# The opening of a fused attention and feed-forward kernel, reordered: a constant built on VectorE, a low part on GpSimd, one weight scaling ahead of a tile's statistics

## What is computed

```python
def reference(x, W_q, W_kv, W_o, gate_w, up_w, down_w, gate_scale, up_scale, down_scale):
    # layernorm: (x - mean) / sqrt(var + 1e-5)
    a = layernorm(x)
    q  = (a @ W_q.T).reshape(B, S, 16, 32)
    kv = (a @ W_kv.T).reshape(B, S, 16, 32)
    qf, kvf = l2_normalize_complex(fft(q)), l2_normalize_complex(fft(kv))
    kvf = cumsum(kvf, axis=1)
    v = ifft(qf * kvf).real.reshape(B, S, D)
    x = x + v @ W_o.T
    f = layernorm(x)
    g = silu((f @ fp8(gate_w)) * gate_scale) * ((f @ fp8(up_w)) * up_scale)
    return x + (g @ fp8(down_w)) * down_scale
```

## Time and profile before

| | |
|---|---|
| median of 3 runs | 422.57 us (422.27 to 423.33) |
| span of the profiled execution | 419.2 us |
| TensorE busy | 411.5 us (98%) |
| VectorE busy | 281.3 us (67%) |
| ScalarE busy | 193.4 us (46%) |
| GpSimd busy | 102.5 us (24%) |
| share of TensorE in the chain that ended last | 95% |

### The profile page before, as it was taken

The page is one execution under the profiler, slowest core; times in us unless marked ns, Lnnn a source line. Parts: engine busy times, 40 slices in busy tenths (PEclk is TensorE's granted clock), DMA queues, the critical chain, the costliest instruction groups (busy, mean ns, idle before and its releaser), DMA issues.

```text
span 419.2 us, 5474 instructions
## 1 busy us (share of the span) xinstructions
PE 411.5 (98%) x1895; PEld 218.8 (52%) x1895; DVE 281.3 (67%) x497; ACT 193.4 (46%) x322; POOL 102.5 (24%) x108
## 2 busy tenths in 40 slices
PE   8999999999999999999999999999999999999994
PEld 4744454455455554554554564454555555555553
DVE  5999998999999694287676952186784744332234
ACT  3787656676755245546222573255342522122220
POOL 0133641015334322045350031043541001300003
PEclk9999999999999999999999999999999999999999
DMA  8986548600381144140112025320112041200002
GB/s 249 289 240 238 177 101 187 141 2 0 94 209 26 38 64 88 39 167 34 27 33 44 2 50 89 62 95 7 25 27 52 0 90 37 75 2 0 2 0 100
DMA packets 57546, 33.54 MB, mean 80 GB/s; under 512 B 49456, under 2 KB 49840, under 8 KB 57392
## 3 DMA queue, kind: packets, MB, share of 16 engines
q1 hardware_dynamic: 57088, 32.93, 30.7%
q10 hardware_dynamic: 432, 0.28, 0.2%
HBM read 17.44 MB, written 4.19 MB: 52 GB/s over the span
## 4 chain that ended last, share of the span: by engine, by line
PE 95%; DMA 1%; DVE 1%; SPq 1%; POOL 0%; POOLq 0%; issue 0%
PE bd L461 21%; PE bu L445 20%; PE bg L445 20%; PE ba L350 15%; PE ba L390 8%; PE bd L350 4%; PE ba L363 1%; DMA h<-x_dram 1%; PE bd L390 1%; PE bd L363 1%; PE bg L350 1%; PE bu L350 1%; PE bu L390 1%; PE bd L407 1%; PE bd L336 0%; PE bg L422 0%
## 5 line engine op out<-in xcount | busy, mean ns | idle before, releaser
L461 PE MATMUL bd<-dw,fu 128*128 128x512 f32 x376 | 100.0, 411 | 0.0
L445 PE MATMUL bu<-hT,gu 128*128 128x512 f16 x384 | 90.7, 379 | 0.0
L445 PE MATMUL bg<-hT,gu 128*128 128x512 f16 x376 | 89.2, 380 | 0.0
L461 PEld LDWEIGHTS bd<-dw,fu 128*128 128x128 f32 x376 | 70.6, 188 | 18.6 <-DVE fu L1165 0.7
L1160 DVE SCALAR_TENSOR_TENSOR ff<-bu,us,sl 128x512 f32<-128x512 f32 x48 | 35.9, 747 | 65.0 <-PE bu L445 61.8
L708 ACT ACTIVATE sl<-bg,gs 128x512 f32<-128x512 f32 x48 | 32.9, 686 | 80.2 <-PE bg L445 79.3
L350 PE MATMUL ba<-wf,xT 128*128 128x512 f16 x288 | 63.2, 379 | 0.0
L445 PEld LDWEIGHTS bu<-hT,gu 128*128 128x128 f16 x384 | 37.4, 98 | 45.6 <-DVE ff L1160 0.6
L445 PEld LDWEIGHTS bg<-hT,gu 128*128 128x128 f16 x376 | 34.1, 98 | 45.8 <-issue 8.9
L1165 DVE TENSOR_TENSOR fu<-ff,fu 128x512 fp32r<-128x512 f32 x47 | 40.1, 856 | 15.7 <-ACT fu L714 15.3
L1534 POOL TENSOR_TENSOR h<-ff,h 128x512 f32<-128x512 f32 x14 | 17.6, 1277 | 129.8 <-DVE ff L1186 129.8
(11 more groups left out here) (180 smaller groups left out, 449.9 us busy)
## 6 DMA issues: line engine op xcount, KB each, us to landing
h<-x_dram SPq DMA_DIRECT2D x16, 256.0 KB, 4.2
out_dram<-h SPq DMA_DIRECT2D x15, 256.0 KB, 2.0
hT<-w_q_dram SPq DMA_DIRECT2D x4, 256.0 KB, 3.8
gu<-w_kv_dram SPq DMA_DIRECT2D x4, 256.0 KB, 4.7
hT<-gate_w_dram SPq DMA_DIRECT2D x2, 512.0 KB, 3.8
hT<-up_w_dram SPq DMA_DIRECT2D x2, 512.0 KB, 5.9
gu<-woT_dram SPq DMA_DIRECT2D x1, 1024.0 KB, 5.5
hT<-down_w_dram SPq DMA_DIRECT2D x2, 512.0 KB, 5.0
```

The lines of the kernel that those rows point to most:

```text
L445: m = e.matmul(bk[:, :], gu[:, c, 4 * w + k, col:col + P], hT[:, b % 2, part, k, :], start=k == 0 and part == 0, stop=k == KT - 1 and part ...
L461: m = e.matmul(bd[t][:, :], fu_at(n)[:, part, P * t:P * t + P], dw[:, i, :], start=i == 0 and part == 0, stop=i == NI - 1 and part == 1)
```

## The change

It does the following, and nothing else:

- `heads` is no longer sent from the host. VectorE builds it after `dve_zero`: one memset of the 128 x 128 square to 0 and four memsets of 32 x 32 squares. The `cst` transfer has 128 instead of 256 columns. The first `pe_heads` waits for these five memsets, the first `dve_head` for the transfer.
- The low part of x's first tile is made by GpSimd (`pool_xl(0, 0)`) instead of VectorE.
- The 4 warm-up matmuls behind the second `pe_heads` are gone.
- On VectorE `dve_head(0, 1)` stands ahead of the statistics of tile 1; those of tile 2 stand behind `dve_head(1, 0)`, those of tile 3 behind `dve_head(1, 1)`.
- On SyncE all four w_kv quarters stand ahead of the transposes of x's first tile, x tile 2 behind them.
- The last waits of SyncE are in another order: those for the outputs of the last batch (d_o[0]) come last, tile 2 at the very end.

The diff, cut to its core:

```diff
-            if j == 0:
-                e.wait_ge(d_cst, 16)
+            if j == 0:
+                e.wait_ge(v_heads, 5)
...
+            if j == 0:
+                e.wait_ge(d_cst, 16)
...
+        def dve_heads(e):
+            e.memset(heads, 0.0).then_inc(v_heads, 1)
+            e.wait_ge(v_heads, 1)
+            for q in range(4):
+                r = slice(HD * q, HD * q + HD)
+                e.memset(cst[r, 128 + HD * q:128 + HD * q + HD], 1.0 / UNIT).then_inc(v_heads, 1)
...
             pe_heads(e, 0, 1)
-            pe_warm(e, 4)
             pe_fold(e, 0, 1)
...
             dve_zero(e)
+            dve_heads(e)
             dve_stats1(e, 0, 0)
...
             dve_head(e, 0, 0)
-            dve_xl(e)
             dve_sum_w(e, 2)
+            dve_head(e, 0, 1)
             dve_stats1(e, 0, 1)
             dve_root0_head(e, 0, [1])
-            dve_head(e, 0, 1)
             dve_root0_tail(e, 0, [1])
             dve_xn(e, 0, 1)
-            dve_stats1(e, 0, 2)
             dve_sum_w(e, 4)
...
             dve_head(e, 1, 0)
-            dve_stats1(e, 0, 3)
+            dve_stats1(e, 0, 2)
             dve_root0_head(e, 0, [2])
             dve_head(e, 1, 1)
+            dve_stats1(e, 0, 3)
             dve_root0_tail(e, 0, [2])
...
         def gpsimd_program(e):
+            pool_xl(e, 0, 0)
             pool_xl(e, 0, 1)
...
             sp_raw(e, 1, 1)
-            sp_x(e, 0, 2)
             sp_raw(e, 1, 0)
-            sp_xT(e, 0, 0)
-            sp_raw(e, 1, 2)
             sp_raw(e, 1, 3)
+            sp_raw(e, 1, 2)
+            sp_xT(e, 0, 0)
+            sp_x(e, 0, 2)
             sp_ident(e)
...
             for t in range(NT):
-                e.wait_ge(d_o[0][t], 16 * 2)
                 e.wait_ge(d_o[1][t], 16)
                 e.wait_ge(d_o[2][t], 16)
+            for t in (0, 1, 3, 2):
+                e.wait_ge(d_o[0][t], 16 * 2)
```

More of the change, by code:

```diff
@@ L39, in constants @@
         inv[r, r] = np.concatenate([ire, iim], 1)
-    heads = np.kron(np.eye(4), np.ones((HD, HD))) / 2.0 ** 14
     ident = np.eye(P)
@@ L43, in constants @@
     ones = np.ones((P, P))
-    return (np.concatenate([fwd, heads, ident], 1).astype(np.float32),
+    return (np.concatenate([fwd, ident], 1).astype(np.float32),
             np.concatenate([inv, tri, ones], 1).astype(np.float32))
+UNIT = 2.0 ** 14
 NPR = 18
@@ L161, in build @@
             sem(n) for n in ("pe_size", "act_size", "act_unit", "dve_size", "dve_inv", "pool_ones"))
+        v_heads = sem("dve_heads")
         a_pT, a_hT, a_silu, a_fu, a_wohi, a_wolo = (sem("act_" + n) for n in ("pT", "hT", "silu", "fu", "wohi", "wolo"))
@@ L165, in build @@
         v_one, v_zero, v_ws, v_head, v_wf = (sem("dve_" + n) for n in ("one", "zero", "ws", "head", "wf"))
-        v_r1, v_xn, v_xl, s_heads = sem("dve_r1"), sem("dve_xn"), sem("dve_xl"), sem("pe_heads")
+        v_r1, v_xn, s_heads = sem("dve_r1"), sem("dve_xn"), sem("pe_heads")
         v_sum, v_mv1, v_n1, v_kn, v_qn, v_T, v_U = (sem("dve_" + n) for n in ("sum", "mv1", "n1", "kn", "qn", "T", "U"))
@@ L284, in x_low_done @@
         def x_low_done(b, t):
-            return (v_xl, 1) if (b, t) == (0, 0) else (p_xl, 4 * b + t)
+            return p_xl, 4 * b + t + 1
         def number(b, t, w):
@@ L1039, in dve_xn @@
                             ALU.mult).then_inc(v_xn, 1)
-        def dve_xl(e):
-            e.wait_ge(a_xh, 1)
-            e.tensor_tensor(xs[:, 0, 1, :], xn[:, 0, :], xs[:, 0, 0, :], ALU.subtract).then_inc(v_xl, 1)
         def dve_refine(e, sem_, at, e_ap, q_ap, y_ap, a_ap, out_ap):
@@ L1657, in sp_cst @@
         def sp_cst(e):
-            e.dma_start(cst[:, 0:256], cst_d).then_inc(d_cst, 16)
+            e.dma_start(fwd, cst_d).then_inc(d_cst, 16)
         def sp_ident(e):
@@ L1683, in sync_program @@
             sp_raw(e, 1, 1)
+            sp_raw(e, 1, 0)
+            sp_raw(e, 1, 3)
+            sp_raw(e, 1, 2)
+            sp_xT(e, 0, 0)
             sp_x(e, 0, 2)
-            sp_raw(e, 1, 0)
-            sp_xT(e, 0, 0)
-            sp_raw(e, 1, 2)
-            sp_raw(e, 1, 3)
             sp_ident(e)
@@ L1826 @@
         "ds": np.ascontiguousarray(L0_ffn_down_scale),
-        "cst": np.ascontiguousarray(cst[:, 0:2 * P]),
+        "cst": np.ascontiguousarray(cst[:, 0:P]),
         "cst2": cst2,
-        "ident": np.ascontiguousarray(cst[:, 2 * P:]),
+        "ident": np.ascontiguousarray(cst[:, P:]),
     }
```

## The result

| | before | changed |
|---|---|---|
| median | 422.56 us (19 runs) | 423.61 us (19 runs, 422.48 to 425.93) |
| ratio, 95% interval | | 1.0036 (1.0023 to 1.0049) |
| a second comparison (12 runs) | | 1.0025 (1.0006 to 1.0044) |
| span of the profiled execution | 419.2 us | 420.5 us |
| first product begins | 13.67 us | 14.54 us |

The change costs 1.5 us by the first ratio, 1.0 us by the second. I had forecast 0.3. The median lies within my range, but a loss of 0.36% was not my case.

A forecast was written before the change was run, and what follows sets the result against it. TensorE's own work was taken to bound the kernel from 13.67 us on. Span 419.2 + 0.43 (VectorE's lateness) - 0.10 (end) = 419.5, plus 3.37 = 422.9 us; range 422.0 to 423.7.

The forecast's parts named there:

- gain at the start, 0.18 us: Opening: the first q/k product would start near 13.49 instead of 13.67 us, 0.18 us earlier, bounds 0 and 0.45.
- VectorE's lateness: Dense part: moved statistics make VectorE 0.45 us late from 25 us, delaying tile 2's triangle product 0.43 to 0.45; chance 0.50.
- the rival I gave 0.10: Before the first product: TensorE's 2.3 us hole lowers the clock, costing 1.7 us, 424.0 us in all; chance 0.10.
- The first transposes: SyncE's queue: they land about 12.9 us, 0.6 to spare, so free; rival that they land late, 423.2 us, chance 0.15.
- The end: SyncE's reordered last waits: five satisfied waits no longer follow the last output, saving 0 to 0.25 us, taken as 0.10.
- The base of the sum: Whole kernel: profiled span 419.2 us, plus 3.37 us to reach the median of 422.57 us.
- second loss: After tile 2's triangle product at 44.7 us: no further loss, TensorE is waited for and all moves together.

The follow-up runs named there:

- before, end's waits: The kernel before with only SyncE's last waits in the changed order: ratio 0.9996 (0.9984 to 1.0008) to the kernel before.
- before once more: The kernel before, unchanged, timed again against itself: ratio 0.9991 (0.9973 to 1.0009).
- before, statistics moved: The kernel before with only the statistics of x's tiles 2 and 3 moved into VectorE's dense part: ratio 1.0011 (0.9996 to 1.0025).
- Filled: The changed kernel with 8 warm-up matmuls in TensorE's hole after the fold of w_q: median 423.00 us, +0.70 ± 0.55 us against the kernel before.
- The kernel with the constant and the end's waits: The kernel before with heads built by VectorE, the smaller constants transfer and the changed order of SyncE's last waits: ratio 1.0012 (0.9998 to 1.0026).
- the kernel that adds GpSimd's part and drops the warm-ups: The changed kernel with second scaling, statistics of tiles 2 and 3 and SyncE's queue back, run twice: ratios 0.9992 and 0.9989 to the kernel before.
- the changed kernel with statistics and queue back: The changed kernel with statistics of tiles 2 and 3 and SyncE's queue where they were before: 423.35 us, ratio 1.0038 (1.0022 to 1.0053).

## Why the prediction was wrong

**The start of the products: the step that failed.** The term "gain at the start, 0.18 us" had the wrong sign. I held that x's second tile lands at 9.17 and that both scalings are done by then, so that putting the second ahead of the statistics gains 0.18 us. Both halves were off. The 9.17 was one execution's: in other traces where the scaling stands behind, the statistics began at 8.21 (before, end's waits), 8.55 (before once more) and 8.97, and in one (before, statistics moved) at 9.17 again. And the second scaling ended not at 9.2 but at 9.8 to 10.8. The 9.2 was too early even by my own rows: the reader at 8.67 and the 0.67 us from a reader to the end of the scalings give 9.34, so little of the 0.18 us was left before anything scattered. The rest has four reasons. The second heads product stands behind the fold of the first quarter on TensorE, and VectorE idles 0.48 to 0.58 us for it; I had it at 8.25, it ran at 9.49 in the changed kernel. The first scaling took 0.97 to 1.22 us instead of 0.48 in three of the nine traces with the scaling ahead, where GpSimd's subtraction ran beside it (0.52 in a fourth). The first heads product, which I had at 6.07, came only when the warm-ups were done, at 7.07 in the changed kernel: they took 6.04 us, and 4.48 to 6.08 over the traces, where I had taken one execution's 4.88. In the two kernels made from before with the scaling ahead alone (6.67) and without the four warm-ups (7.18) it waited for the sum over the second quarter of w_q, which landed at 5.8 and 6.3 us there and at 4.8 in the earlier trace rows's execution. What VectorE awaits in front of the statistics it can no longer do while the tile is under way. Over the nine traces with the scaling ahead (without the one whose statistics waited for a tile) the first product begins at 13.81 to 14.80, 14.35 in the mean, over the eight with it behind at 13.12 to 14.33, 13.72: **+0.63 us, give or take 0.4, not -0.18**. Some 0.2 us of it may be the draw: the first heads product came at 6.87 in the mean of the nine and at 6.66 in the eight.

**VectorE's lateness: borne out.** I had 0.63 us (0.83 less the 0.20 of slack) before taking off the gain of the start. From the first product to the triangle product of tile 2 it is 31.52 to 32.69 us with the statistics moved (eight traces, mean 31.97) and 31.02 to 31.97 without (eight, mean 31.28; the two traces in which the clock fell are left out): 0.69 us, give or take 0.4. The path was the one I named, but for its last step (ScalarE's copy of `wo` in place of GpSimd's low part). The size in time, 0.45 ± 0.48 us alone, agrees, though by itself it hardly excludes nothing at all. The landing of x tile 1 of batch 1 scatters by about a us as well, which is why single traces overlap.

**The clock: the rival I gave 0.10.** The two falls seen in traces are those of the kernels with holes of 2.1 and 3.3 us; in the changed kernel the falls are read from the mean clocks. The four warm-ups were free by my account, since they lie off the path; they delayed the fold and so shortened the hole behind it. The size of the effect was right: 1.7 us forecast for one fall, 4.37 - 2.75 = 1.62 us measured. That is in part luck: I took it from the 14 warm-ups of one execution, 4.88 less 3.2 us, and over the traces the same sum gives 1.3 to 2.9. What I mis-sized was whether it happens. I took it as one outcome for all executions; it is a chance in each. With holes of 0.8 to 1.3 us none of 120 timed executions of nine kernels is low, with 2.0 to 2.1 us unfilled 21 of 61 are, with 3.3 us 5 of 6. Filled, 0 of 12. In the changed kernel it adds 12/31 of 1.3 us, 0.5 us. The only fall in the trace of before came 3.7 us after the last matmul, and I read that as how long a hole must be; in the trace above the clock fell after a hole of 2.1 us, and with TensorE at work again. So how long a hole must be was read from a single fall, and that reading failed. The Trainium skill, "TensorE: Matmul & The Clock Gate" (What you observe and What's actually happening), has the throttled state as the default that activity lifts, and gives a moment of transition that differs from run to run. The runs agree with both: the first warm-up matmuls stand 0.43 us apart, and they close up near 3.8 us in one trace and only near 7.0 in another (last section).

**The first transposes: right that they are free.** The second was issued near 8.6 in the changed kernel and took 3.8 us, so it landed near 12.4; in the traces shown here VectorE's low part of the weights released the first product.

**The end: too small a term.** 0.10 us taken, 0.35 measured, so 0.07 us for each of the five waits, where I had the 0.05 between two issues as the most.

**The sum, with what was measured:** 0.63 (start) + 0.69 (lateness) + 0.5 (clock) - 0.35 (end) = 1.5 us, against 1.45 and 1.00 us. The first two are differences of traces, not of times; in times scaling and statistics together cost 0.80 ± 0.40. With 0.4 us of play in each of the two, that the sum comes out at 1.5 is better than it had a right to.

**The base of the sum.** I added 3.37 us to the span as what lies around it. In all 327 executions for which both are on record, the time exceeds the span by 1.75 to 2.00 us. So the profiled execution of the kernel before took about 421.1 us, 1.4 under the median, and its rows are those of a short execution. The difference that I forecast does not hang on this, but each landing that I took from it does.

**What stays open.** A part of the scatter comes from behind the triangle product, where I had seen no second loss. Near 100 us TensorE waits for ScalarE in 11 of 18 traces, for 0.15 to 1.00 us. In the second trace of the kernel before:

```profile
92.77 0.61 ACTq L679 DMA_DIRECT2D qk<-qk  x1
...
96.40 1.80 POOL L1514 TENSOR_TENSOR qk<-qk 1x512 f32<-1x512 f32 x1 [6.05 <-DMA qk<-qk]
...
98.24 0.63 ACT L671 ACTIVATE ks<-qk 128x512 f16<-128x512 f32 x1 [3.69 <-POOL qk L1514]
...
99.41 0.69 ACT L708 ACTIVATE sl<-bg,gs 128x512 f32<-128x512 f32 x1
...
100.24 1.89 PE L445 MATMUL bg<-hT,gu 128*128 128x512 f16 x8 [1.00 <-ACT sl L708]
```

A 2 KB transfer that carries the running sum to the next tile lands 2.9 to 3.7 us after its issue, GpSimd's addition behind it takes 1.25 to 1.80 us, and ScalarE, which works in order, holds its other work until then. In the first trace of that kernel it was 3.0 and 1.26 us, and TensorE did not wait. The wait is in 3 of 7 traces of kernels made from the one before and in 8 of 11 of those made from the changed one; whether the change has a part in it, no run shows.

The kernel with the constant and the end's waits was 0.49 ± 0.42 us slower than before where I expected 0.3 faster, while the two runs of the kernel that adds GpSimd's part and drops the warm-ups were 0.5 faster. And the changed kernel with statistics and queue back should have gained on the changed one and did not (+1.58 ± 0.57). Differences of 0.5 us are at the edge of these comparisons, and the landing of w_q's second quarter (4.7 to 6.6 us over the traces, its mean 5.2 in seven traces with the large transfer of constants and 5.7 in eleven with the small one, which may or may not be chance) moves the opening by as much. I don't settle them.

## What to carry to other kernels

On an engine that works in order, an instruction that waits for another engine belongs behind the work whose input has already landed; where a transfer's landing scatters, take its earliest, not the one execution's. Before dummy matmuls are removed as off the path, look at how long TensorE then idles before it is needed: the price is paid in some of the executions only, so one clean trace proves nothing, and the mean granted clock of many executions shows it. When work moves out of a hole into a stretch with no slack, it costs its duration, less what slack is left, at the next point where the two engines meet (0.69 us here for 0.83 us of work and 0.20 of slack).

## What the runs showed of the hardware that I had not expected

- Two scalings of 128x128 fp32 on VectorE took 0.48 us, but 0.52 to 1.22 us when they began while GpSimd ran a subtraction of two 128x512 tiles. In all seven such traces they ended 0.27 to 0.29 us after the subtraction (7.20 + 1.16 = 8.36 against 7.66 + 0.97 = 8.63 in the changed kernel), as if held until it was done. The Trainium skill, "GPSIMD Engine Reference" (Key points), says that GpSimd shares its SBUF interfaces with VectorE and contends with instructions in a 2-port mode or with two inputs there; the runs agree that the two contend, and give the price, but do not tell which of these conditions it was.
- The 14 warm-up matmuls at the start took 4.48 to 6.08 us over the traces, and their weight loads stand 0.43 us apart until the clock rises: up to 3.72 us in the trace with the shortest warm-up, up to 6.29 us in the one with the longest. Behind the rise a matmul of this size takes about 0.22 us, so a rise that comes one us later costs half a us, and the 1.6 us mean that the rise moved by some 3 us between executions (an estimate: from 3.8 to 7.0 us).
- A wait of SyncE that is already satisfied cost 0.07 us (0.35 us for five).
- The same 2 KB transfer landed 2.9 to 3.7 us after its issue over the traces, and the last output of 256 KB at 2.6 us in 16 traces and 3.5 in two.
